# The last chunk's attention results by way of device memory, an earlier read of the last but one's, and one output block moved behind the last probabilities-times-values step

## The reference

```
styles = w @ (affine_w * gain).T + affine_b          # one factor per input feature and batch
y = einsum('blc,oc->blo', x * styles, weight) * dcoefs   # L0, then + bias and clip to +-256
kx = modulated_linear(x, s, k_aff_w, k_aff_b, k_w, k_b)  # K; q = k = v = kx
scores = einsum('bnhd,bnjd->bnhj', q, k) / sqrt(32)      # 16 x 16 per token
out = einsum('bnhj,bnjd->bnhd', softmax(scores), v)
out = modulated_linear(out, s, o_aff_w, o_aff_b, o_w, o_b)  # O
x = x + L0(x);  x = x + O(attention(K(x)))
```

## Time and profile before

| | us |
|---|---|
| median of three runs | 706.44 |
| lowest, highest | 705.59, 707.33 |
| profiled execution | 709.13 |
| its span (first to last instruction or landing) | 705.5 |
| PE busy | 687.1 (97%) |
| DVE busy | 580.1 (82%) |
| ACT busy | 544.5 (77%) |

### The profile page before, as it was taken

One profiled execution on the slowest core, in us unless ns is written; L12 is line 12 of the kernel. 1 busy time (PEld: TensorE's weight loads), 2 busy tenths in 40 slices (PEclk: granted clock), 3 DMA queues, 4 the chain that ended last, 5 costly groups with the idle time before them and its releaser, 6 DMA issues.

```text
span 705.5 us, 21689 instructions
## 1 busy us (share of the span) xinstructions
PE 687.1 (97%) x8904; PEld 669.5 (95%) x8904; DVE 580.1 (82%) x1049; ACT 544.5 (77%) x1073; POOL 114.0 (16%) x105
## 2 busy tenths in 40 slices
PE   9999999999999999999999999999999999999767
PEld 8999999999999999989999999999999999999767
DVE  4689987888988889878889988888988789988853
ACT  6898977878777788677888777788777788777854
POOL 2021311111110111101111101111110111103000
PEclk9999999999999999999999999999999999999998
DMA  8467978578867677777767876777776768867763
GB/s 291 130 179 197 223 191 233 154 206 223 224 164 208 198 202 222 168 203 200 202 197 221 221 196 171 205 206 212 210 198 177 196 204 219 210 180 211 183 178 119
DMA packets 229394, 139.85 MB, mean 198 GB/s; under 512 B 141488, under 2 KB 222896, under 8 KB 229296
## 3 DMA queue, kind: packets, MB, share of 16 engines
q1 hardware_dynamic: 228144, 138.21, 72.1%
q10 hardware_dynamic: 1152, 0.26, 0.2%
HBM read 71.33 MB, written 66.58 MB: 195 GB/s over the span
## 4 chain that ended last, share of the span: by engine, by line
PE 57%; DMA 13%; ACT 12%; DVE 8%; SPq 5%; issue 3%; ACTq 0%; DVEq 0%; POOL 0%; POOLq 0%
PE lin_ps L451 46%; DMA yr<-y_turned 6%; PE s_ps L503 5%; PE y_ps L521 4%; DMA k_turned<-kx 3%; DMA y_turned<-y 3%; ACT kx L545 3%; ACT y_hi L554 2%; SPq L264 2%; ACT p_bd L649 2%; SPq L288 2%; ACT x_hi L554 2%; SPq L280 1%; DVE x L830 1%; PE s_ps L461 1%
## 5 line engine op out<-in xcount | busy, mean ns | idle before, releaser
L451 PE MATMUL lin_ps<-x_hi,w_hi 128*128 128x256 f32 x1008 | 286.6, 285 | 2.2 <-ACT x_hi L554 1.5
L451 PE MATMUL lin_ps<-x_lo,w_hi 128*128 128x256 f32 x1008 | 280.8, 279 | 0.0
L451 PE MATMUL lin_ps<-x_hi,w_lo 128*128 128x256 f32 x1008 | 280.5, 279 | 0.0
L451 PEld LDWEIGHTS lin_ps<-x_hi,w_hi 128*128 128x128 f32 x1008 | 189.1, 188 | 11.9 <-issue 6.9
L420 POOL COPY k_bd<-k_rhs 32x1024 f32<-32x1024 f32 x94 | 109.7, 1167 | 545.4 <-DVE k_rhs L805 541.7
L451 PEld LDWEIGHTS lin_ps<-x_lo,w_hi 128*128 128x128 f32 x1008 | 189.2, 188 | 0.0
L451 PEld LDWEIGHTS lin_ps<-x_hi,w_lo 128*128 128x128 f32 x1008 | 189.2, 188 | 0.0
L554 ACT ACTIVATE x_hi<-x,style 128x256 fp32r<-128x256 f32 x252 | 113.1, 501 | 65.2 <-DVE x L830 59.5
L451 PE MATMUL lin_ps<-y_hi,w_hi 128*128 128x256 f32 x528 | 150.0, 284 | 7.1 <-DVE y_lo L748 6.8
L748 DVE SCALAR_TENSOR_TENSOR x_lo<-x,style,x_hi 128x256 fp32r<-128x256 f32 x252 | 145.0, 627 | 12.4 <-ACT x_hi L554 12.4
L451 PE MATMUL lin_ps<-y_lo,w_hi 128*128 128x256 f32 x528 | 149.2, 283 | 0.0
(11 more groups left out here) (65 smaller groups left out, 734.3 us busy)
## 6 DMA issues: line engine op xcount, KB each, us to landing
k_st<-k_turned SPq DMA_DIRECT2D x128, 128.0 KB, 3.2
v_turned<-k_rhs SPq DMA_DIRECT2D x32, 512.0 KB, 6.1
k_v<-v_turned SPq DMA_DIRECT2D x128, 128.0 KB, 3.6
x<-xT SPq DMA_DIRECT2D x31, 512.0 KB, 5.7
k_turned<-kx SPq DMA_DIRECT2D x31, 512.0 KB, 2.9
y_turned<-y SPq DMA_DIRECT2D x124, 128.0 KB, 3.3
yr<-y_turned SPq DMA_DIRECT2D x31, 512.0 KB, 4.7
outT<-o SPq DMA_DIRECT2D x29, 512.0 KB, 4.2
```

Of the source, the lines that this page charges most:

```text
L451: mm = pe.matmul(lin_ps[:, (n + j) % NLB, 0:T], w[:, k, (m + j) * P:(m + j + 1) * P], r[:, k, :], start=(q == 0), stop=(q == len(passes) - 1))
```

## The change

Four things are changed, all of them in the tail.

1. Chunk 31's results go through device memory like all others, but into `yr_last`. SP and ACT issue two of the four writes each (`y_to_dram(last, range(HR // 2))`, `results_to_dram`). `last_y_from_dram` on SP waits for all four and reads back in two halves of 256 KB, each with its own semaphore; `y_hi_of(last, h)` waits for its own half. This takes the place of the 16 small copies.
2. On SP, `y_from_dram(last - 1)` stands ahead of store 27 instead of behind it, and the writes and the read of chunk 31 stand ahead of it too.
3. On PE, block 3 of O 28 is moved behind `pv(31)`.
4. On ACT, blocks 1 and 2 of O 28 are evacuated ahead of the high parts of chunk 29, and block 3 behind the writes of chunk 31. On DVE, `sums(31)` goes in between the two halves of `y_lo_of(28)`, and `finish(26, 1)` ahead of the low parts of chunk 29.

```
-            + blocks(O, last - 4, [2, 3]) + one("scores", last) + one("pv", last - 1) + blocks(O, last - 3)
-            + one("pv", last) + blocks(O, last - 2) + blocks(O, last - 1) + blocks(O, last))
+            + blocks(O, last - 4, [2, 3]) + one("scores", last) + one("pv", last - 1) + blocks(O, last - 3, [0, 1, 2])
+            + one("pv", last) + blocks(O, last - 3, [3]) + blocks(O, last - 2) + blocks(O, last - 1) + blocks(O, last))
...
-            def results_over(c, js):
-                sp.wait_ge(a_y, 2 * (c + 1))
-                sp.wait_ge(k_out_landed, DMA * c)
-                for j in js:
-                    for g in range(HEADS // KB):
-                        sp.dma_start(yr_last[HD * g:HD * (g + 1), :, j * TB:(j + 1) * TB],
-                                     y_sb[HD * j:HD * (j + 1), g::HEADS // KB, :, :].rearrange("p n l s -> p n (l s)")
-                                     ).then_inc(y_last_landed, DMA)
+            def last_y_from_dram():
+                sp.wait_ge(y_out_landed, DMA * HR * N)
+                sp.wait_ge(k_out_landed, DMA * last)
+                for h in range(2):
+                    ks = slice(h * KB // 2, (h + 1) * KB // 2)
+                    sp.dma_start(yr_last[:, ks], y_dram[last % 2].rearrange("(k p) t -> p k t", p=P)[:, ks]).then_inc(
+                        y_last_landed[h], DMA)
...
+            y_from_dram(last - 1)
+            y_to_dram(last, range(HR // 2))
+            last_y_from_dram()
             store(last - 4, 0, 1)
-            y_from_dram(last - 1)
-            results_over(last, range(HR // 2))
...
-                    act.wait_ge(y_last_landed, DMA * HR * HEADS // KB)
+                    act.wait_ge(y_last_landed[h], DMA)
...
-            def results_over(c):
+            def results_to_dram(c):
                 act.wait_ge(a_y, 2 * (c + 1))
-                act.wait_ge(k_out_landed, DMA * c)
+                act.wait_ge(y_in_landed, DMA * (c - 1))
                 for j in range(HR // 2, HR):
-                    for g in range(HEADS // KB):
-                        act.dma_start(yr_last[HD * g:HD * (g + 1), :, j * TB:(j + 1) * TB],
-                                      y_sb[HD * j:HD * (j + 1), g::HEADS // KB, :, :].rearrange("p n l s -> p n (l s)")
-                                      ).then_inc(y_last_landed, DMA)
+                    act.dma_start(y_dram[c % 2].rearrange("(n d) t -> d n t", d=HD)[:, :, j * TB:(j + 1) * TB],
+                                  y_sb[HD * j:HD * (j + 1), :, :, :].rearrange("p n l s -> p n (l s)")
+                                  ).then_inc(y_out_landed, DMA)
```

More of the change, by code:

```diff
@@ L152, in build @@
         y_out_landed, y_in_landed = sem("y_out_landed"), sem("y_in_landed")
-        y_last_landed = sem("y_last_landed")
+        y_last_landed = [sem(f"y_last_landed{h}") for h in range(2)]
         st_o = [sem(f"st_o{i}") for i in range(2)]
@@ L281, in v_from_dram, with y_to_dram @@
                                  src[:, :, ct]).then_inc(v_in_landed, DMA)
-            def y_to_dram(c):
+            def y_to_dram(c, js=range(HR)):
                 sp.wait_ge(a_y, 2 * (c + 1))
@@ L286, in y_to_dram @@
                     sp.wait_ge(y_in_landed, DMA * (c - 1))
-                for j in range(HR):
+                for j in js:
                     sp.dma_start(y_dram[c % 2].rearrange("(n d) t -> d n t", d=HD)[:, :, j * TB:(j + 1) * TB],
@@ L729, in _ @@
                 (last - 1, evacuate_y, 0), (last - 1, evacuate_y, 1), (last - 3, o_out, 0), (last, spread_some, 0),
-                (last, spread_some, 1), (last, spread_some, 2), (last, spread_some, 3), (last - 2, y_hi_of, 0),
-                (last - 2, y_hi_of, 1), (last - 3, o_out, 1), (last - 3, o_out, 2), (last - 3, o_out, 3),
-                (last, evacuate_y, 0), (last, evacuate_y, 1), (last, results_over), (last - 2, o_out, 0),
+                (last, spread_some, 1), (last, spread_some, 2), (last, spread_some, 3), (last - 3, o_out, 1),
+                (last - 3, o_out, 2), (last - 2, y_hi_of, 0), (last - 2, y_hi_of, 1), (last, evacuate_y, 0),
+                (last, evacuate_y, 1), (last, results_to_dram), (last - 3, o_out, 3), (last - 2, o_out, 0),
                 (last - 1, y_hi_of, 0), (last - 1, y_hi_of, 1), (last - 2, o_out, 1), (last - 2, o_out, 2),
@@ L911, in _ @@
                 (last - 1, normalise), (last - 1, spread_probabilities), (last - 1, turn_v), (last, merge_scores),
-                (last, subtract_maxima), (last - 3, y_lo_of, 0), (last - 3, y_lo_of, 1), (last, sums),
-                (last, normalise), (last, spread_probabilities), (last, turn_v), (last - 2, y_lo_of, 0),
-                (last - 2, y_lo_of, 1), (last - 5, finish, 1), (last - 4, finish, 0), (last - 4, finish, 1),
+                (last, subtract_maxima), (last - 3, y_lo_of, 0), (last, sums), (last - 3, y_lo_of, 1),
+                (last, normalise), (last, spread_probabilities), (last, turn_v), (last - 5, finish, 1),
+                (last - 2, y_lo_of, 0), (last - 2, y_lo_of, 1), (last - 4, finish, 0), (last - 4, finish, 1),
                 (last - 3, finish, 0), (last - 3, finish, 1), (last - 1, y_lo_of, 0), (last - 1, y_lo_of, 1),
```

## The result

| | kernel before | changed kernel |
|---|---|---|
| median us (executions) | 705.44 (12) | 701.62 (12) |
| lowest us | 703.57 | 699.27 |
| ratio of the two, 95% interval | | 0.9936 [0.9913, 0.9959] |
| profiled execution: its time, its span | 709.13, 705.5 | 703.06, 701.3 |
| mean granted clock of the profiled execution | 0.995 | 0.998 |

The change makes the kernel faster by 0.64%, some 4.5 us (2.9 to 6.1 by the interval). Forecast were 5.6 us and 700.8.

The account below looks back on a forecast made before the run. PE's 6.0 us wait in front of O 30, some 3.3 of it SP's order, and the low clock behind it were taken as the bound. Earlier O 30 3.8 + clock 1.8 = 5.6 us off 706.44 gave 700.8 us, range 699.3 to 703.9.

Parts of the forecast that it names:

- The bound: PE's wait of 6.01 us in front of O 30; some 3.3 us of it are SP's order.
- Softmax of chunk 31 on DVE: Chunk 28's second low parts 0.27 us late, chunk 31's normalising and values 0.83 us early; pv(31) at 673.57.
- The moved block gains PE nothing: O 28 [3] behind pv(31) on PE gains nothing by itself; PE waits about 0.7 us for values, before 0.41.
- yr 30 issued 3.0 us earlier: Read of chunk 30 on SP: issued at 677.02, landing in 5.36 us, O 30 3.8 us earlier (3.0 to 5.1).
- Round robin between queues: By this rule ACT's two writes of chunk 31 share with yr 30, whose landing would be 6.2 us, not 5.36.
- The last results hidden behind O 30: Chunk 31's writes and half reads in front of O 31 cost 0; by the upper bound 0.6 us.
- The rival on the slower side: Chunk 31's results come late and the clock falls in front of O 31: 709.1 us; chance 0.05.
- The clock: PE's clock stays up through a 1.6 us gap in front of O 30: 1.8 us gained, bounds 0 and 1.8.
- The first rival: The clock falls all the same in front of O 30: 702.6 to 703.4 us; chance 0.21.
- the likeliest case: Tail from O 30 on: earlier read and clock staying up, 5.6 us gained, 700.8 us; chance 0.60.
- The median: Whole kernel: 5.6 us off the median of three runs, 706.44, gives 700.8 us.

Follow-up runs that it names:

- e1_read_first: Kernel before with one edit: on SP, the read of chunk 30's results and the small copies stand ahead of store 27; 0.9977 of the kernel before.
- e10_finish_back: Changed kernel with finish(26, 1) alone back behind the low parts of chunk 29 on DVE; 0.9977 of the kernel before.
- after_again: The changed kernel itself, timed a second time in another group; 0.9933 of the kernel before.
- after_third: The changed kernel itself, timed a third time as reference for the last group; 0.9929 of the kernel before.
- e9_block_back_again: Changed kernel with O 28 [3] back ahead of pv(31) on PE, ACT's evacuations back too, run again; 0.9919 of the kernel before.
- e2_small_copies: Changed kernel with chunk 31's results copied straight by 16 small transfers, 8 on SP and 8 on ACT; 0.9960 of the kernel before.
- e5_fill_before: Kernel before with 44 filling matmuls in PE's idle time ahead of O 30; 0.9969 of the kernel before.
- e6_fill_after: Changed kernel with 14 filling matmuls ahead of pv(30) and 12 ahead of O 30; 0.9910 of the kernel before.
- e8_block_back_fill: Changed kernel with O 28 [3] back ahead of pv(31), plus 14 and 12 filling matmuls; 0.9906 of the kernel before, median 697.97 us.
- e3_block_back: Changed kernel with O 28 [3] back ahead of pv(31) on PE, ACT's evacuations back too, first run; 0.9901 of the kernel before.
- e4_dve_back: Changed kernel with both moves on DVE undone, chunk 31's sum and reciprocal and finish(26, 1); 0.9971 of the kernel before.

## Why the prediction was right, point by point

- **The bound.** Right. Much of PE's wait in front of O 30 was SP's order. I had put 3.3 us of the 6.0 down to it, with both stores. With store 27 alone out of the way (e1_read_first) O 30 starts 1.9 us earlier; the other part is store 26, which e10_finish_back puts at 1.1 us of waiting and more in the read itself.
- **Softmax of chunk 31 on DVE.** Right in size. In the changed kernel `pv(31)` starts 8.61 us behind `pv(30)`, although the clock was low for a part of it, in after_again 8.02 and in after_third 8.27; before it was 9.34. Forecast was 8.5. In the first of these profiles the last thing it waited for was ACT's share of the spread, which I had ending before the values.
- **The moved block gains PE nothing.** Right: e9_block_back_again against after_third.
- **yr 30 issued 3.0 us earlier.** On the count 2.9, 3.9 and 2.9 in the three profiles of the changed kernel. Its landing: 5.6, 5.4 and 5.7 for 5.36 forecast. O 30 starts 3.5, 4.7 and 3.4 us earlier, for 3.8 forecast.
- **Round robin between queues.** The Trainium skill, "DMA: Bandwidth & Descriptors", section on queues, rings and completion order, says that each transfer engine goes round the queues it has work for. By that rule ACT's two writes would have shared with the read, which I had put at 6.2 us. The changed kernel's traces speak against that size: with ACT's writes going out 0.1 to 0.2 us behind it the read took 5.4 to 5.7, and with eight of ACT's copies beside it (e2_small_copies) 5.6. They don't settle the rule. Beside other transfers the read never was quicker than 4.9, where the shortest of the seven in the trace before took 4.0, and the two long ones, 6.8 and 6.9, had both ACT's writes and store 26 ahead of them. A store close ahead in its own queue isn't enough by itself (5.7 in e1_read_first). What made the 6.19 us of the kernel before is open: e5_fill_before, with the same order on SP and ACT, took 5.7.
- **The last results hidden behind O 30.** Right, with less room than forecast. All four writes were down at 685.02, 19.0 us behind `pv(30)` where I had 17.1, since SP's second write was held 2.6 us in issue and the slowest landing was 6.0 us, not 4.2:

```profile
L288 SPq DMA_DIRECT2D y_turned<-y x2: 451/1524/2598, 678.5 to 679.0; - x2
...
DMA to landing us min/median/max: 4.4/4.9/6.0
```

  The two half reads made it good. They land in 2.9 and 3.2 us, where I had only bounds from whole reads:

```profile
L304 SPq DMA_DIRECT2D kx<-y_turned x2: 377/425/473, 685.0 to 685.4; - x2
...
DMA to landing us min/median/max: 2.9/3.1/3.2
```

  The second half was there at 685.4 + 3.2 = 688.6; ACT turned to it at 689.29, as soon as it had evacuated O 30 [1]. That is 0.7 us of cover. The rival on the slower side would have needed an O 31 as late as 693.8; it started at about 691.3.
- **The clock: the mis-sized term.** I counted 1.8 us in full, on the ground that the new gap of 1.6 us is shorter than one of 2.12 that left the clock up. The term was right for the profiles of the changed kernel and of after_again (11.61 and 11.71 us for the 96 matmuls) and wrong for after_third, where the clock fell in the gap in front of O 30, of 2.22 us, and the 96 matmuls took 12.90:

```profile
681.89:684.11 2.22, 0.00 (x1) 0.03 (x1) 1.03 (x3) 1.97 (x5) 0.00 (x0) 0.93 0.05 12
684.11:687.00 2.89, 2.89 (x13) 2.89 (x14) 1.25 (x3) 1.09 (x3) 0.00 (x0) 0.50 0.78 260
```

  In e9_block_back_again it fell behind a gap of 1.86 us, in the changed kernel's profile behind the unchanged one of 2.12 in front of `pv(30)`. The first rival was not an alternative to the likeliest case, but something that happens to some executions of the same kernel. The mean of the three is 1.2 us gained in O 30 and O 31 in place of 1.8, and part of that is given back in front of `pv(30)` where the clock falls there. The first of these is as large as the 0.6 us between 5.6 forecast and the 5.0 on the count, though four single profiles can't show that it is the cause. The timed 4.5 us, with an interval of 2.9 to 6.1, tell nothing finer.
- **The median.** 700.8 against 701.62 looks closer than the gain was. I took the 5.6 us off 706.44, while the kernel before came to 705.44 in the comparison. The two medians lie 3.8 us apart, 1.8 less than forecast, and the lower start made up for 1.0 of them by luck.

What stays open: how the 4.5 us divide. The parts don't add up, because they are one chain. Undoing the DVE move takes away some 3 us and undoing the way through device memory some 2, the read alone brings 1.6 to 2.2, and the clock's 1.2 to 1.6 come only when the gap is short enough.

## What to carry to other kernels

When an engine waits for a read, look at what stands in front of the read in its issuing queue, and at the one small instruction on another engine for which that waits: in e10_finish_back a sum of 0.65 us held a store and the store a read, and O 30 came 2.3 us later, with the clock down. Copies issued by ACT held it for 0.7 to 0.9 us each (8 in 5.5 to 7.2 us), so a longer way with fewer issues can be the faster one. And where PE's gaps can't be closed, harmless matmuls in them kept its clock up here: 0.999 to 1.000 in all twelve executions of e6_fill_after and e8_block_back_fill.

## What the runs showed of the hardware that I had not expected

- The same idle gap of PE does not always do the same to its clock. Eleven profiles have the gap of 2.12 us in front of `pv(30)` with nothing in it and the clock up ahead of it: in four (changed kernel, e1_read_first, e3_block_back, e5_fill_before) the clock fell to 0.50 at its end or within 1.3 us behind it, in seven it stayed. In front of O 30, gaps of 1.86 us (e9_block_back_again) and 2.22 us (after_third) brought 0.50, one of 1.85 us (changed kernel) did not. The 69 executions of the kernel before have clocks from 0.989 to 0.998, none at 1.000.
- The clock is not all that spreads the times of one kernel: at 0.999 to 1.000 the six executions of e6_fill_after lie from 697.26 to 703.07 us. What else does is open.
- A read of 512 KB issued 0.5 us behind a store of 512 KB on the same queue was held 1.4 to 2.8 us in issue (e1_read_first, e4_dve_back, e10_finish_back); with the store 2.0 to 3.6 us ahead it was 0.38 us. It landed after 5.7, 6.9 and 6.8 us, against 4.9 to 5.7. With the store 1.2 to 1.4 us ahead (e5_fill_before, kernel before) it was held 0.7 us and landed after 5.7 and 6.2.
- `pv(30)`, which no kernel here moves, starts anywhere between 661.2 and 668.2 us. One source is in the profiles, PE's wait for the last keys, 0.6 us in most and 1.7 to 2.4 in four. It explains less than 2 of the 7 us; the rest arises further ahead. A span is thus no measure of a change in the tail; a count from a common point is a better one.
